# Latent attention on one core: queries from one product per group, with the rotated partners in eight unused rows of each head

## What is computed

```
cq  = x @ W_DQ                      # 64 latent values per token
ckv = x @ W_DKV                     # 64
q_h = [cq @ W_UQ (16),  rope(cq @ W_QR) (8)]      for each of 16 heads
k_h = [ckv @ W_UK (16), rope(x @ W_KR) (8)]       the rotated part is shared by all heads
p   = causal softmax(q_h . k_h / sqrt(24));  out_h = p @ (ckv @ W_UV)
rope(a)[2j]   = a[2j] cos - a[2j+1] sin
rope(a)[2j+1] = a[2j+1] cos + a[2j] sin
```

## Time and profile before

| what | value |
|---|---|
| median of 3 runs | 3048.02 us (3040.27 to 3054.22) |
| the profiled execution's own time | 3047.79 us |
| its span, first to last instruction | 3045.9 us |
| mean granted TensorE clock | 0.963 |
| TensorE busy | 2770.7 us (91%) |
| DVE busy | 1627.9 us (53%) |
| ACT busy | 1213.3 us (40%) |
| POOL busy | 1077.0 us (35%) |

### The profile page before, as it was taken

How to read it: one execution, slowest core, us unless ns; L and a number is a source line. 1 busy time by engine, 2 the same in 40 slices (tenths; PEclk the granted TensorE clock), 3 DMA queues, 4 the chain that set the end, 5 groups by cost and what they waited for, 6 DMA issues and landing times.

```text
span 3045.9 us, 42333 instructions
## 1 busy us (share of the span) xinstructions
PE 2770.7 (91%) x15646; PEld 1863.9 (61%) x15646; DVE 1627.9 (53%) x3890; ACT 1213.3 (40%) x2265; POOL 1077.0 (35%) x767
## 2 busy tenths in 40 slices
PE   6999999999999899999989898999988899999992
PEld 3565656556565656555555555555554488999992
DVE  6656566575656456676676768585754520000003
ACT  4444444535344444444444544444543232222221
POOL 5423243343423233353444535353532321111113
PEclk8999999999999999999999999999998799999996
DMA  3000000000001011001010101010000367999886
GB/s 134 11 23 17 25 28 25 15 25 15 25 22 46 25 40 59 20 5 49 4 49 4 49 4 42 11 39 15 29 15 31 132 233 268 343 357 344 326 325 206
DMA packets 85767, 261.72 MB, mean 86 GB/s; under 512 B 10653, under 2 KB 49901, under 8 KB 66877
## 3 DMA queue, kind: packets, MB, share of 16 engines
q1 hardware_dynamic: 79084, 241.25, 21.9%
q0 software_dynamic: 6480, 17.77, 1.5%
HBM read 210.68 MB, written 44.11 MB: 84 GB/s over the span
## 4 chain that ended last, share of the span: by engine, by line
PE 73%; DVE 12%; issue 4%; DMA 4%; POOL 3%; ACT 3%; SPq 1%; POOLq 0%; DVEq 0%; ACTq 0%
PE s_pD L703 20%; PE s_pA L703 17%; PE s_pD L1155 7%; PE s_pA L1140 6%; PE s_pD L860 3%; PE s_pA L753 3%; PE s_pD L775 3%; PE s_pA L762 3%; DMA s_w_w<-rows_s 3%; DVE s_pairs L1735 2%; PE s_pA L742 2%; DVE s_qk L1634 2%; PE s_pA L870 2%; ACT s_qk L1209 1%; PE s_pD L941 1%
## 5 line engine op out<-in xcount | busy, mean ns | idle before, releaser
L1456 POOL TENSOR_TENSOR s_qk<-s_qk,s_rrec 128x1024 f32<-128x1024 f32 (+1 forms) x128 | 215.7, 1685 | 578.0 <-DVE s_rrec L1640 577.9
L1209 ACT ACTIVATE s_qk<-s_qk,s_mx 128x256 f32<-128x256 f32 (+1 forms) x512 | 239.9, 469 | 341.0 <-DVE s_mx L1634 340.3
L703 PE MATMUL s_pA<-s_w_wqkv,s_curT 128*128 128x512 f32 x768 | 354.3, 601 | 5.6 <-ACT s_curT L1185 3.7
L703 PEld LDWEIGHTS s_pA<-s_w_wqkv,s_curT 128*128 128x128 f32 x768 | 142.4, 191 | 176.6 <-issue 163.1
L1735 DVE TENSOR_SCALAR s_pairs<-s_pD 128x1024 f32<-128x1024 f32 (+1 forms) x192 | 194.4, 1038 | 103.9 <-PE s_pD L860 101.1
L2086 DVE COPY s_w_wo<-s_pD 128x256 f32<-128x256 f32 x71 | 30.0, 423 | 409.6 <-PE s_pD L1126 409.6
L1555 POOL DMA_INDIRECT acc_s<-s_w_w,s_sq x71 | 68.3, 962 | 458.9 <-ACT s_w_w L1397 451.6
L1450 POOL TENSOR_TENSOR s_rinv<-s_ssq,s_half 128x16 f32<-128x16 f32 x64 | 207.5, 3242 | 5.1
L860 PE MATMUL s_pD<-s_mixer 32*128 32x512 f32 (+3 forms) x1024 | 186.4, 477 | 23.6 <-DVE s_pairs L1735 18.5
L1446 POOL TENSOR_TENSOR s_qk<-s_qk,s_rot 128x1024 f32<-128x1024 f32 x64 | 150.5, 2351 | 135.5 <-DVE s_qk L1617 135.4
L703 PE MATMUL s_pA<-s_zT,s_w_w 128*120 128x512 f32 (+1 forms) x384 | 186.7, 609 | 1.1 <-ACT s_zT L1225 1.1
(11 more groups left out here) (276 smaller groups left out, 5922.9 us busy)
## 6 DMA issues: line engine op xcount, KB each, us to landing
s_qkT<-in_m_w SPq DMA_DIRECT2D x48, 1024.0 KB, 5.2
s_v_tm<-in_m_w SPq DMA_DIRECT2D x24, 1024.0 KB
s_rot<-in_m_w SPq DMA_DIRECT2D x24, 1024.0 KB, 5.1
s_w_wqkv<-in_m_w SPq DMA_DIRECT2D x23, 1024.0 KB
s_qk<-in_m_w SPq DMA_DIRECT2D x23, 1024.0 KB, 6.1
s_w_w<-rows_s SPq DMA_DIRECT2D x71, 129.0 KB
s_cur<-in_x SPq DMA_DIRECT2D x8, 512.0 KB, 3.5
xn_s<-s_cur SPq DMA_DIRECT2D x8, 512.0 KB, 2.8
```

The lines of the kernel that those rows point to most:

```text
L703: last = nc.tensor.matmul(out, lhs(c), rhs(c), start=(c == 0), stop=(c == n - 1))
L1209: last = nc.scalar.activation(pi, pi, ACT.Exp, scale=-1.0, bias=mx[:, u, i:i + 1], accum_out=rsum[:, u, i:i + 1])
L1456: nc.gpsimd.tensor_tensor(pi, pi, rrec[:, u, :].unsqueeze(2).broadcast_to((P, 4, 256 - lo)), ALU.mult).then_inc(p_rdy, 1)
```

## The change

The second product of the queries goes. Its weights (the partners) now fill the eight rows of each head that were zero, so that one product gives, per head, 16 content rows, 8 plain rotated rows and 8 partner rows. One table lqt (ones, cosines, signed sines) multiplies all of it in one DVE instruction straight into QT. The sum of the two parts is now made by the scores themselves, whose contraction runs over all 32 rows of a head: the shared key stands in both groups of eight rows. For that the key's weights and tables lcos and lsin are filled in both places, and keep the same shapes.

So per group: one product instead of two on the lower rows, and the key's product is written first; one DVE instruction instead of two; no POOL sum and no semaphore lq_rdy. The queries' PSUM job takes one bank. Scores wait for DVE's instruction. The shared key is computed in place in KrT with a scratch of 512 columns. In stage 8 SP loads lqt (256 KB) as one more table, behind a wait for the last retention gates (its place was theirs); the joint table lWqk is 768 columns wide instead of 1024.

```diff
-WIDE = ("qkT", "S", "qk", "PT", "kr", "lq", "sc", "AT", "ro")
+WIDE = ("qkT", "S", "qk", "PT", "kr", "sc", "AT", "ro")
...
-        W["lWqk"] = part(mixer, 9480, 1024, i=2, g=LG, n=P)
+        W["lWqk"] = part(mixer, 9480, 768, g=LG + 2, n=P)
...
-        rm = part(mixer, 2048, 1024, i=2, n=T)
+        rm = part(mixer, 2048, 512)
+        W["lqt"] = part(mixer, 2560, 512)
...
                         for n in lat_weights:
                             sp.dma_start(W[n], I["w_" + n]).then_inc(lat_in, 16)
+                        sp.wait_ge(og_rdy, NT * B)
+                        sp.dma_start(W["lqt"], I["w_lqt"]).then_inc(lat_in, 16)
                     sp.dma_start(s_tm[:], S["s"][b]).then_inc(xs_in, 16)
...
             def keys_queries(b, g):
                 pe.wait_ge(outD, doneD["lat", b])
                 ps = slotD("kc", b, g)
                 pq = slotD("lq", b, g)
-                nc.tensor.matmul(pq[:, 0:T], W["lWqk"][0:LAT, 0, g, :], latT[0:LAT, :], start=True, stop=True)
-                nc.tensor.matmul(ps[:, 0:T], W["lWqk"][LAT:P, 0, g, :], latT[LAT:P, :], start=True, stop=True).then_inc(mmD, 1)
-                nc.tensor.matmul(pq[:, T:2 * T], W["lWqk"][0:LAT, 1, g, :], latT[0:LAT, :], start=True, stop=True).then_inc(mmD, 1)
+                nc.tensor.matmul(ps[:, 0:T], W["lWqk"][LAT:P, g, :], latT[LAT:P, :], start=True, stop=True).then_inc(mmD, 1)
+                nc.tensor.matmul(pq[:, 0:T], W["lWqk"][0:LAT, g, :], latT[0:LAT, :], start=True, stop=True).then_inc(mmD, 1)
...
             def last_queries():
-                pq = slotD("lq", LAST, 3)
-                nc.tensor.matmul(pq[:, 0:T], W["lWqk"][0:LAT, 0, 3, :], latT[0:LAT, :], start=True, stop=True)
-                nc.tensor.matmul(pq[:, T:2 * T], W["lWqk"][0:LAT, 1, 3, :], latT[0:LAT, :], start=True, stop=True).then_inc(mmD, 1)
+                nc.tensor.matmul(slotD("lq", LAST, 3)[:, 0:T], W["lWqk"][0:LAT, 3, :], latT[0:LAT, :], start=True, stop=True).then_inc(mmD, 1)
...
             def latent_scores(b, w, rounds):
                 g, pr = w // 2, w % 2
-                pe.wait_ge(lq_rdy, LG * b + g + 1)
+                pe.wait_ge(outD, doneD["lq", b, g])
...
-            def query_sum(b, g):
-                pool.wait_ge(outD, doneD["lq", b, g])
-                nc.gpsimd.tensor_tensor(QT[:, g % 2, :], rm[:, 0, :], rm[:, 1, :], ALU.add).then_inc(lq_rdy, 1)
-
...
             def shared_key(b):
                 ps = take("kr", b)
-                if b:
-                    dve.wait_ge(lq_rdy, LG * b)
-                nc.vector.tensor_tensor(rm[:, 0, :], ps[:, 0:T], W["lcos"], ALU.mult)
-                nc.vector.tensor_tensor(rm[:, 1, :], ps[:, T:2 * T], W["lsin"], ALU.mult).then_inc(outD, 1)
+                nc.vector.tensor_tensor(KrT, ps[:, 0:T], W["lcos"], ALU.mult)
+                nc.vector.tensor_tensor(rm, ps[:, T:2 * T], W["lsin"], ALU.mult).then_inc(outD, 1)
                 dve.wait_ge(outD, doneD["kr", b])
-                step(nc.vector.tensor_tensor(KrT, rm[:, 0, :], rm[:, 1, :], ALU.add))
+                step(nc.vector.tensor_tensor(KrT, KrT, rm, ALU.add))
...
             def queries(b, g):
                 ps = take("lq", b, g)
-                if g:
-                    dve.wait_ge(lq_rdy, LG * b + g)
-                nc.vector.tensor_tensor(rm[:, 0, :], ps[:, 0:T], W["lcos"], ALU.mult)
-                nc.vector.tensor_tensor(rm[:, 1, :], ps[:, T:2 * T], W["lsin"], ALU.mult).then_inc(outD, 1)
+                nc.vector.tensor_tensor(QT[:, g % 2, :], ps, W["lqt"], ALU.mult).then_inc(outD, 1)
```

42 lines of the change are left out of this document (19 added, 23 removed).

## The result

The changed kernel takes **3054.1 us** (median of 20 runs, 3044.8 to 3062.9) against 3047.9 us of the kernel before (20 runs). The ratio is 1.0025, with a 95% interval of 1.0014 to 1.0035. The forecast was 3036, and 3054 lies outside its range. The difference is within the 0.5% that I called no change, but on the slow side, and its interval leaves out even a small gain: some 18 us are missing against the forecast.

What follows compares the result with a forecast made beforehand. TensorE was taken as the bound: 73% of the chain of waits, busy for 91% of the span. Gains of 4.1 + 0.7 + 0 + 4.4 + 2.0 + 0.9 = 12.1 us gave 3036, range 3023 to 3048.

Steps and rivals of the forecast that it cites:

- 155.4 us instead of 156.8: Sign that the forecast is right: length of a stage at clock 1.00 after the change, against before.
- u = 5, group 0: Key and query products of group 0: gain taken as 0, with 7 us kept for the range.
- u = 6 and u = 8: Products before the scores, stages 8 to 14: gains of 0.58 and 0.1 us, seven times each, 4.1 and 0.7 us.
- The variant with 0.09 at u = 6: Key's eviction from PSUM as the only limit: gain 0.09 instead of 0.58 us there, sum 8.7 instead of 12.1.
- Group 3: Value products right behind the pair in stages 9 to 14: 0.73 us earlier, six times, 4.4 us.
- The margin of 0.2 us before the DMA: Start of a stage: DVE's 0.93 us wait for TensorE's scores takes in the 0.73 and leaves 0.2.
- Stage 15 and the routed phase: Three shorter waits at half clock, 2.0 us, and the last group's removed product, 0.9 us.
- the clock's scatter of some 8 us: Whole kernel: uncertainty of some 8 us that the forecast itself carries from TensorE's clock.
- rival C: Stages 9 to 14 all go like the slowest: 21.9 us more, less 12.1, giving 3058; chance 0.08.
- C's trigger: Covered time before the scores at u = 6 and u = 8 turns into waits of some 0.8 us.
- B: Each lone product's TensorE time counts in full across stages and end: 21.5 us gained, 3026; chance 0.17.
- D: Key first keeps key and query products apart; group 0 loses 0.88, about 3 us gained in sum, 3045; chance 0.12.

Runs made afterwards that it cites:

- 3 fillers: Changed kernel plus 10, 9 and 6 identity products inside TensorE's waits of 2.64, 2.40 and 1.51 us: 3028.2 us; the kernel before with them: 3038.5.
- one filler: Changed kernel plus only the 10 identity products of 128 columns ahead of the 2.64 us wait: 3040.3 us, 0.9978 of before.
- the pad: Changed kernel with 832 columns of a gate product done twice in stages 9 to 14: 3059.8 us, 1.0048 of before.
- the two at 1.40 us: Pairs of groups 1 and 2 ahead of the local value products, three fillers, plus two of 5 products before probability transposes: 3026.4 us, 0.9928 of before.
- two fillers inside waits: Kernel before plus 9 identity products ahead of the latent projections and 6 ahead of group 2's value products: 3045.0 us, 0.9999 of before.
- earlier products: Changed kernel with the key and query products of groups 1 and 2 ahead of the local value products, stages 8 to 14: 3039.1 us, 0.9971 of before.

## Why the prediction was wrong

**The sum of the work was right in the stages.** The pieces of a stage, measured between the first products of the groups (at u = 5 the key's) and compared where the clock is full on both sides:

| piece | gain predicted | before | changed | gain |
|---|---|---|---|---|
| group 3 to u = 5 | 0.73 | 116.65 | 115.92 (3 fillers) | 0.73 |
| u = 5 to u = 6 | 0 | 3.97 | 3.92 | 0.05 |
| u = 6 to u = 8 | 0.58 | 13.40 | 12.92 | 0.48 |
| u = 8 to the next group 3 | 0.1 | 22.82 | 22.65 | 0.17 |
| stage | 1.41 | 156.84 | 155.41 | 1.43 |

The "155.4 us instead of 156.8" of the prediction is thus 155.41, though no stage of the changed kernel itself ran at full clock throughout: the first piece, at full clock, exists only in versions with a filler ahead of the 2.64 us wait. The fillers themselves don't lengthen it: the kernel before takes 115.80 us from group 3 to the first product of u = 5 without them and 115.82 with three. The other pieces are the changed kernel's own, the last from stages 11 and 13. With their counts (seven, eight or six times) these gains make 9.3 us, where the prediction had 9.2.

**u = 5, group 0:** taken at 0, measured 0.05; the bound of 0.88 for a late query didn't come.

**u = 6 and u = 8:** the wait was put at 0.79 and is 0.87, so the gain up to u = 8 is 0.48 instead of 0.58; behind u = 8 it is 0.17 instead of 0.1. The variant with 0.09 at u = 6 (sum 8.7) is out.

**Group 3:** right to 0.01 us, but with some luck. L869 came 0.83 us earlier, not 0.73 (the recorded subtraction itself gives 0.75). The margin of 0.2 us before the DMA was not there: in each of the six stages DVE's 0.93 us are gone, and the shifted rows by DMA are what it waits for (1.8 to 2.2 us). Its next step behind the clips (L1605, before L1615) stands 0.59 to 0.78 us earlier after the stage's start. So the DMA does limit this gain; it happens to do so at 0.73, and by these rows a larger saving here would not have been kept.

**Stage 15 and the routed phase** (2.9 us expected): from the first product of group 3 in stage 15 to the end, the profiles have 3045.9 - 2283.7 = 762.2 us before and 3045.4 - 2290.3 = 755.1 after. It is 7.1 us less, more than twice what was expected. Of this 1.0 lies between group 3 and u = 5, where I took 0, and 1.2 between u = 5 and u = 6, where I took 0.6. Another 3.3 us are shorter waits for expert rows (12.6 against 15.9 in the whole profile; the 14.3 of the earlier trace rows are its part from 2434 on) and 1.9 a smaller loss to the clock (the parts overlap a little). With one profile each, the last two may be scatter: with three fillers the same stretch takes 761.8 us changed and 763.0 before, a difference of 1.2. So the 2.9 us are neither confirmed nor refuted.

**The step that failed** is in "How the numbers follow": "The forecast itself carries the clock's scatter of some 8 us". I took what the clock takes as noise around a mean that the change leaves where it is. It isn't: the loss went from 107 to 132 us in the mean over all runs, 25 us more, against 17 less left. In the two profiles the falls in stages 9 to 14 cost 15.7 us more time than before, and the work saved was 8.6. The result is rival C in its sign, by the mechanism that C had named ("in some stages TensorE falls to 1.2 GHz for a while after short waits, in others not"). That it lies within 4 us of C's 3058 is luck: C had all six stages go like the slowest, at 163.35, and one did. It got a chance of 0.08, and the range left it out. My reason against it was that idle time hardly grows and that "stages with the same small waits keep the full clock". The second half was the warning, read the wrong way round: if the same waits sometimes bring a fall and sometimes don't, then something else has a part in it, and an edit that moves the waits may change it. And before had something to lose: two stages of 156.8 us without a fall, one of them in the earlier trace rows.

C's trigger, the new waits, is neither confirmed nor ruled out. They are not needed for falls: the version with the product issued twice has none of them and loses 122. They are not enough: with three fillers the changed kernel keeps them and loses 94, and the largest lever found is a wait of 2.64 us which is as long before as after. But falls that make the piece from u = 6 to u = 8 longer by 3 us or more stand only in profiles of kernels that have the 0.87 us: in two of six stages of the changed kernel, three with the query first, four with the product removed only, one with one filler. The four profiles of the kernel before, with and without fillers, have none there; the product twice has two of 1.5 us, behind another wait.

**B** (3026) is refuted by the 0.87 us waits, which keep the lone products from counting in full. **D** (3045) is refuted by the pair's records and by the version with the query first.

The Trainium skill, TensorE: Matmul & The Clock Gate, section Part 1: The HAM clock gate (the "warmup" mystery), says that the counting behind the clock gate runs freely and isn't restarted by the kernel. The traces agree with the consequence: the same 2.64 us wait behind the same work has a fall behind it in one stage and none in another. The section speaks of its effect on the start of a kernel. That this counting decides where the clock falls in the middle of one would fit these runs, but none of them shows it.

**What stays open.** Which phase of a stage is a good one: neither the old length (the pad) nor a filled wait (the two at 1.40 us) could be relied on. And the ledger is rough: two fillers inside waits took 14 us of loss from the kernel before and nothing from its time (3045.0), so its "left" rose from 2937 to 2950 with no work on the path. The argument for the saving rests on the clean pieces, not on 2919 against 2937, nor on one pair of filled kernels. Open, too, is what share the new waits of 0.87 us have in the falls.

## What to carry to other kernels

Before costing an edit on TensorE, look at the granted clock of each stage; if the same stage runs in several lengths, then the clock is a term of the sum, in which the edit's own microseconds can be outweighed either way (here -12 of work came out as +6, and -6 as -15). Compare versions by work and clock separately, piece by piece where both run at the full clock, before a change is called useless. The same fillers in both are a weaker test: here they turned +6 us into +7, -10 or -25, by their number. And a filler belongs into a bank that is free *during* the wait; one in the bank that is being waited for only lengthens it.

## What the runs showed of the hardware that I had not expected

- Removing one TensorE product per group, with the remaining query written behind the key, made the kernel 0.56% slower (3064.8), with stages of 163.6 to 163.8 us from stage 11 on, at a clock of 0.93 to 0.95.
- Ten products of 128 columns in a wait of 2.64 us, in stages 9 to 14, that compute nothing are worth 14 us (3054.1 to 3040.3); three fillers in a version with earlier products bring 21 by the medians (3039.1 to 3017.7), 16 by the ratios (0.9971 to 0.9920).
- Two 64-row products of 512 columns that run on the two row halves took from 1446.56 to 1447.69, 1.13 us for both, where the record of one alone, L842 of before, is 1.02 us long (0.88 of it behind the pair): side by side they cost little more than one, and the version with the query first shows the same pair.
